# Dense attention of layer 0: head 0's row maxima as a + relu(b - a), differences issued a tile ahead, three relu buffers

## The reference

```python
mod = (_silu(L0_c) @ L0_wmod).reshape(L0_c.shape[0], 6, 1, -1)
h = _layernorm(x, axis=-1) * (1 + ca) + sa
x = x + ga * _L0_attn_ref(h, L0_attn_W_query, L0_attn_W_key, L0_attn_W_val, L0_attn_W_out)
...
        norm = 1.0 / np.sqrt(KEY_DIM)
        Q = jnp.einsum('bsd,hdk->hbsk', q, W_query)
        K = jnp.einsum('bsd,hdk->hbsk', q, W_key)
        V = jnp.einsum('bsd,hdv->hbsv', q, W_val)
        scores = norm * jnp.einsum('hbqk,hbnk->hbqn', Q, K)
        attn = jax.nn.softmax(scores, axis=-1)
        heads = jnp.einsum('hbqn,hbnv->hbqv', attn, V)
        out = jnp.einsum('hbqv,hve->bqe', heads, W_out)
...
```

## Time and profile before

| what | value |
|---|---|
| median of three runs | 1733.46 us |
| the profiled execution's own time | 1726.0 us |
| its span in the trace | 1724.2 us |
| VectorE busy | 1303.6 us (76%) |
| TensorE busy | 1239.0 us (72%) |
| ScalarE busy | 889.7 us (52%) |
| GpSimd busy | 236.1 us (14%) |

### The profile page before, as it was taken

One profiled execution on the slowest core, in us unless ns is written; L12 is line 12 of the kernel. 1 busy time (PEld: TensorE's weight loads), 2 busy tenths in 40 slices (PEclk: granted clock), 3 DMA queues, 4 the chain that ended last, 5 costly groups with the idle time before them and its releaser, 6 DMA issues. The chain is left out here.

```text
span 1724.2 us, 29793 instructions
## 1 busy us (share of the span) xinstructions
PE 1239.0 (72%) x10670; PEld 619.8 (36%) x10674; DVE 1303.6 (76%) x3511; ACT 889.7 (52%) x1757; POOL 236.1 (14%) x275
## 2 busy tenths in 40 slices
PE   7799999999999997574993453060215989824686
PEld 3122222222222223354982342040113547623445
DVE  6999999999999972447237236989897568578873
ACT  4099999999999996412521122020002775502553
POOL 2000000000000000003410324030003321000223
PEclk9599999999999999667995586565656988965668
DMA  2100000011000000000004331000001721031001
GB/s 73 37 14 27 21 21 21 22 28 28 23 21 20 21 2 2 15 29 1 1 1 188 101 84 46 0 0 1 1 0 27 228 68 43 4 116 49 22 22 31
DMA packets 45030, 62.88 MB, mean 36 GB/s; under 512 B 12785, under 2 KB 34356, under 8 KB 44484
## 3 DMA queue, kind: packets, MB, share of 16 engines
q1 hardware_dynamic: 38243, 49.71, 9.7%
q0 software_dynamic: 5440, 10.67, 2.3%
q10 hardware_dynamic: 1200, 0.59, 0.1%
HBM read 34.10 MB, written 13.63 MB: 28 GB/s over the span
## 5 line engine op out<-in xcount | busy, mean ns | idle before, releaser
L842 ACT ACTIVATE l0att_probs<-l0att_ps_sv 128x512 f32<-128x512 f32 x960 | 521.2, 596 | 80.0 <-PE l0att_ps_sv L811 68.1
L888 DVE TENSOR_REDUCE l0att_half_negmax<-l0att_ps_m 128x1 f32<-128x1024 f32 x480 | 547.1, 1216 | 5.6 <-PE l0att_ps_m L741 5.6
L773 PE MATMUL l0att_ps_sv<-l0att_probs,l_V_aug 128*32 128x256 f32 x4096 | 325.3, 392 | 4.8 <-ACT l0att_pv_sb L833 4.7
L811 PE MATMUL l0att_ps_sv<-l_Q,l_K 51*128 51x512 bf16 x992 | 194.5, 388 | 4.0 <-ACT l0att_probs L850 2.4
L741 PE MATMUL l0att_ps_m<-l_K,l_Q 48*128 48x512 bf16 x960 | 185.9, 384 | 11.1 <-DVE l0att_half_negmax L888 7.1
L773 PEld LDWEIGHTS l0att_ps_sv<-l0att_probs,l_V_aug 128*32 128x32 f32 x4096 | 83.0, 108 | 197.4 <-issue 100.9
L811 PEld LDWEIGHTS l0att_ps_sv<-l_Q,l_K 51*128 51x128 bf16 x992 | 48.0, 92 | 207.4 <-ACT l0att_probs L842 188.1
L472 POOL CAST l0att_nm<-l0att_negmax 128x16 bf16<-128x16 f32 x16 | 3.2, 198 | 515.0 <-DVE l0att_negmax L864 515.0
L2862 ACT ACTIVATE l3loc_probs<-l3loc_ps_s 128x320 f32<-128x320 f32 x128 | 48.9, 435 | 36.0 <-PE l3loc_ps_s L2839 35.3
L2040 DVE SCALAR_TENSOR_TENSOR l2spk_lif_v<-l2spk_U 128x64 f32<-128x64 f32 (+1 forms) x368 | 60.8, 207 | 0.0
L741 PEld LDWEIGHTS l0att_ps_m<-l_K,l_Q 48*128 48x128 bf16 x960 | 47.1, 95 | 28.5 <-DVE l0att_half_negmax L888 19.0
(11 more groups left out here) (736 smaller groups left out, 2391.8 us busy)
## 6 DMA issues: line engine op xcount, KB each, us to landing
l_K<-l_kp SPq DMA_DIRECT2D x192, 32.0 KB
l_Q<-l_qp SPq DMA_DIRECT2D x192, 32.0 KB
l1ffn_W<-in_l_expert_w_dram SPq DMA_DIRECT2D x1, 4096.0 KB
l3f_experts_l_w<-in_l_w_dram SPq DMA_DIRECT2D x2, 2048.0 KB
l_sorted_in<-l1ffn_zeros SPq DMA_DIRECT2D x1, 3072.0 KB
l1exp_rows<-l_sorted_in SPq DMA_DIRECT2D x6, 512.0 KB, 5.6
l_sorted_out<-l1exp_y SPq DMA_DIRECT2D x6, 512.0 KB, 4.6
l_Q<-in_local_mask_q_dram POOLq DMA_DIRECT2D x2, 1170.0 KB, 17.3
```

Of the source, the lines that this page charges most:

```text
L773: mm = pe.matmul(ps_v[32 * c:32 * c + 32, cols], V_aug[:, kt, h, :], probs[:, kt % 2, c, cols], start=(kt == 0 and part == 0), stop=(kt == ...
L811: pe.matmul(dst, K[at, h % HEAD_BUFS, c1(kt)], Q[at, h % HEAD_BUFS, c4(2 * pair + i)], start=True, stop=True).then_inc(last_scored[i] if l ...
L842: act.activation(probs[:, kt % 2, c, :], ps_s[:, n % 3, :], ACT.Exp).then_inc(expd, 1)
L888: dve.tensor_reduce(half_negmax[:, h % 2, t, half:half + 1], src, AX_X, ALU.max, negate=True).then_inc(m_read, 1)
```

## The change

Three things are done. First, for query tiles 1 to 15 of head 0, the maximum over the two halves is taken as max(a, b) = a + relu(b - a): TensorE makes b - a in one product over 112 rows of new operands (`Q_both` holds Q and, 64 rows further, -Q; `K_both` holds the keys of the upper half and, 64 rows further, those of the lower half; rows 32 to 63 are cleared first, and 32 to 47 filled again), ScalarE takes the relu into SBUF, and VectorE adds the scores a of the lower half to it and reduces the sum in the same instruction (`tensor_tensor_reduce`). Tile 0 is made as before, with two reductions. The difference of tile u + 1 is issued ahead of the lower scores of tile u, and the relu has three buffers. Second, SyncE loads head 1's rows ahead of the second copy of head 0's. Third, TensorE multiplies the identity by itself five times at the start of the block. GpSimd clears the rows between in the stage ahead.

```diff
@@ stage_project_parts, gpsimd
                 pool.memset(V_aug[:, :, :, L0_K:L0_K + 1], 1.0).then_inc(v_filled, 1)
+                pool.wait_ge(v_filled, 2)
                 if beside is not None:
                     beside(pool)
                 rows_finish(pool, g)
-                pool.wait_ge(v_filled, 2)
@@ stage_l0_attend
+        above = st.sb("above", [P, 3, S // 2])
...
-        first_scores = [ps_m[:, 0, :], ps_m[:, 1, :], ps_sv[:, 0:2, :].rearrange("p b n -> p (b n)"),
-                        ps_sv[:, 2:4, :].rearrange("p b n -> p (b n)")]
+        first_low = [ps_m[:, 0, :], ps_sv[:, 0:2, :].rearrange("p b n -> p (b n)")]
+        first_diff = [ps_m[:, 1, :], ps_sv[:, 2:4, :].rearrange("p b n -> p (b n)")]
@@ sync
-                for piece in high:
-                    load_piece(sp, Q, K, qp, kp, 0, loaded_high, *piece)
                 for h in range(1, L0_H):
...
                         load_piece(sp, Q, K, qp, kp, h, loaded[h % HEAD_BUFS], *piece)
+                    if h == 1:
+                        for piece in high:
+                            load_piece(sp, Q, K, qp, kp, 0, loaded_high, *piece)
@@ tensor
-                pe.wait_ge(loaded_first, LOAD // 2)
-                for n in range(2 * NT):
-                    t, half = n // 2, n % 2
-                    if n >= 4:
-                        pe.wait_ge(first_read, n - 3)
-                    for i in range(2):
-                        pe.matmul(first_scores[n % 4][:, i * BANK:(i + 1) * BANK], Q[0:TERMS, 0, c1(t)],
-                                  K[0:TERMS, 0, c4(2 * half + i)], start=True, stop=True).then_inc(first_filled, 1)
-                pe.wait_ge(first_read, 2 * NT)
+                def first_plain(half):
+                    for i in range(2):
+                        mm = pe.matmul(first_low[half][:, i * BANK:(i + 1) * BANK], Q[0:TERMS, 0, c1(0)],
+                                       K[0:TERMS, 0, c4(2 * half + i)], start=True, stop=True)
+                    mm.then_inc(low_filled, 1)
+                def first_difference(u):
+                    if u >= 2:
+                        pe.wait_ge(above_done, u - 1)
+                    for i in range(2):
+                        mm = pe.matmul(first_diff[u % 2][:, i * BANK:(i + 1) * BANK], Q_both[:, c1(u + 1)],
+                                       K_both[:, c4(i)], start=True, stop=True)
+                    mm.then_inc(diff_filled, 1)
+                def first_lower(u):
+                    pe.wait_ge(low_read, u + 1)
+                    for i in range(2):
+                        mm = pe.matmul(first_low[u % 2][:, i * BANK:(i + 1) * BANK], Q[0:TERMS, 0, c1(u + 1)],
+                                       K[0:TERMS, 0, c4(i)], start=True, stop=True)
+                    mm.then_inc(low_filled, 1)
+                keep_busy(pe, g, first_diff[1], 5)
+                for operand in loaded_first:
+                    pe.wait_ge(operand, LOAD // 4)
+                for half in range(2):
+                    first_plain(half)
+                pe.wait_ge(both_placed, 4)
+                first_difference(0)
+                for u in range(NT - 1):
+                    if u + 1 < NT - 1:
+                        first_difference(u + 1)
+                    first_lower(u)
+                pe.wait_ge(low_read, NT + 1)
@@ scalar
+                act.wait_ge(loaded_first[0], LOAD // 4)
+                act.activation(Q_both[0:TERMS, :], Q[0:TERMS, 0, :], ACT.Identity).then_inc(both_placed, 1)
+                for u in range(NT - 1):
+                    act.wait_ge(diff_filled, u + 1)
+                    if u >= 3:
+                        act.wait_ge(low_read, u)
+                    act.activation(above[:, u % 3, :], first_diff[u % 2], ACT.Relu).then_inc(above_done, 1)
@@ vector
-                for n in range(2 * NT):
-                    dve.wait_ge(first_filled, 2 * (n + 1))
-                    dve.tensor_reduce(half_negmax[:, 0, n // 2, n % 2:n % 2 + 1], first_scores[n % 4], AX_X, ALU.max,
-                                      negate=True).then_inc(first_read, 1)
+                dve.memset(half_negmax[:, 0, 1:NT, 1], -LOWEST).then_inc(missing_set, 1)
+                dve.wait_ge(loaded_first[1], LOAD // 4)
+                dve.tensor_copy(K_both[0:TERMS, :], K[0:TERMS, 0, S // 2:S]).then_inc(both_placed, 1)
+                dve.tensor_copy(K_both[HALF_ROWS:HALF_ROWS + TERMS, :], K[0:TERMS, 0, 0:S // 2])\
+                   .then_inc(both_placed, 1)
+                dve.wait_ge(loaded_first[0], LOAD // 4)
+                dve.tensor_scalar(Q_both[HALF_ROWS:HALF_ROWS + TERMS, :], Q[0:TERMS, 0, :], -1.0, None,
+                                  ALU.mult).then_inc(both_placed, 1)
+                for half in range(2):
...
+                for u in range(NT - 1):
+                    dve.wait_ge(low_filled, u + 3)
+                    dve.wait_ge(above_done, u + 1)
+                    dve.tensor_tensor_reduce(above[:, u % 3, :], first_low[u % 2], above[:, u % 3, :], -1.0, -LOWEST,
+                                             ALU.add, ALU.min, half_negmax[:, 0, u + 1, 0:1]).then_inc(low_read, 1)
@@ layer0_attention
+        def clear_between(pool):
+            for n, operand in enumerate((Q_both, K_both)):
+                pool.memset(operand[32:HALF_ROWS, :], 0.0).then_inc(both_cleared, 1)
+                pool.wait_ge(both_cleared, n + 1)
```

More of the change, by code:

```diff
@@ L615, in load_piece, with stage_l0_attend @@
     eng.dma_start(operand[at:at + TERMS - 5:6, h % HEAD_BUFS, :], parts[part][h:P:L0_H, :]).then_inc(landed, 16)
-def stage_l0_attend(nc, loads, g, V_aug, qp, kp, Q, K, ones_placed, loaded_first, O):
+def stage_l0_attend(nc, loads, g, V_aug, qp, kp, Q, K, ones_placed, loaded_first, Q_both, K_both, O):
     LEAD = 4
@@ L658, in stage_l0_attend @@
         nm_placed = [st.sem("nm_placed0"), st.sem("nm_placed1")]
-        first_filled = st.sem("first_filled")
-        first_read = st.sem("first_read")
+        both_placed = st.sem("both_placed")
+        low_filled = st.sem("low_filled")
+        low_read = st.sem("low_read")
+        diff_filled = st.sem("diff_filled")
+        above_done = st.sem("above_done")
+        missing_set = st.sem("missing_set")
         negmax_ready = st.sem("negmax_ready")
@@ L874, in normalise @@
                                       ALU.mult).then_inc(m_read, 1)
[L876 to L879 removed]
+                dve.memset(half_negmax[:, 0, 1:NT, 1], -LOWEST).then_inc(missing_set, 1)
[7 more added lines that the diff above has]
+                for half in range(2):
+                    dve.wait_ge(low_filled, half + 1)
+                    dve.tensor_reduce(half_negmax[:, 0, 0, half:half + 1], first_low[half], AX_X, ALU.max,
+                                      negate=True).then_inc(low_read, 1)
+                for u in range(NT - 1):
[3 more added lines that the diff above has]
+                                             ALU.add, ALU.min, half_negmax[:, 0, u + 1, 0:1]).then_inc(low_read, 1)
                 for i, what in enumerate(turns):
@@ L954, in layer0_attention @@
         ones_placed = st.sem("ones_placed")
-        loaded_first = st.sem("loaded_first")
+        loaded_first = [st.sem("loaded_first_q"), st.sem("loaded_first_k")]
+        both_cleared = st.sem("both_cleared")
+        Q_both = st.sb("Q_both", [HALF_ROWS + TERMS, S], BF16)
+        K_both = st.sb("K_both", [HALF_ROWS + TERMS, S // 2], BF16)
         for half in range(2):
@@ L966, in first_rows @@
                 if (SPLITS_Q, SPLITS_K)[which][r] == part:
-                    load_piece(sp, Q, K, qp, kp, 0, loaded_first, 0, r, which)
-        stage_project_parts(nc, for_parts, "l0_wqkv", g, 0, "l0proj", V_aug, qp, kp, rows_of_part=first_rows)
-        stage_l0_attend(nc, for_attend, g, V_aug, qp, kp, Q, K, ones_placed, loaded_first, O)
+                    load_piece(sp, Q, K, qp, kp, 0, loaded_first[which], 0, r, which)
+        def clear_between(pool):
+            for n, operand in enumerate((Q_both, K_both)):
+                pool.memset(operand[32:HALF_ROWS, :], 0.0).then_inc(both_cleared, 1)
+                pool.wait_ge(both_cleared, n + 1)
+        stage_project_parts(nc, for_parts, "l0_wqkv", g, 0, "l0proj", V_aug, qp, kp, beside=clear_between,
+                            rows_of_part=first_rows)
+        stage_l0_attend(nc, for_attend, g, V_aug, qp, kp, Q, K, ones_placed, loaded_first, Q_both, K_both, O)
         stage_project_out(nc, for_out, "l0_wout", g, "l0out", O, mod_row(g, 0, GATE_A))
```

3 lines of the change are left out of this document (2 added, 1 removed).

## The result

| | kernel before | changed kernel |
|---|---|---|
| median, first measurement | 1732.06 us (1725.74 to 1736.72, 4 runs) | 1711.88 us (1705.01 to 1722.01, 4 runs) |
| median, second measurement | 1731.53 us (1722.99 to 1734.77, 11 runs) | 1712.89 us (1708.85 to 1715.46, 6 runs) |
| ratio, first and second | | 0.990 (0.9871 to 0.9929), 0.9901 (0.9875 to 0.9926) |

A forecast was written before the change was run, and what follows sets the result against it. VectorE was taken to bound head 0's maxima; their end moving from 71.52 to 56.9 us gains 14.6, the rest costed at nothing, so the median of 1733.46 becomes 1718.9 us, range 1714 to 1729.

The forecast's parts named there:

- What bounds the kernel: Head 0's maxima: VectorE bounds this part, 32 reductions at 1.13 us each from start to start, 36.30 us in all.
- The new start: Opening of the attention stage: first reduction at 36.4 us, 1.2 later than before; first combined instruction at 38.65.
- The bound from below: First reduction of head 0: nothing is gained past 36.0 us, when the first plain scores arrive.
- The tiles: Head 0's 15 tiles: 1.21 us each (bounds 1.13 and 1.25), ending at 56.9 in place of 71.52, a gain of 14.6.
- TensorE at the lower clock: Head 0's tiles: TensorE becomes the bound at 1.71 us a tile, end 64.1, gain 7.4, time 1726.1; chance 0.30.
- Its milder form: Head 0's tiles: TensorE regains its clock after some 7 us, gain 11.9, time 1721.6; shares the lower-clock rival's chance of 0.30.
- The slow instruction: Head 0's tiles: combined instruction as slow as the scan, 2.28 us a tile, time 1734.9; chance 0.05.
- The loads: Head 1's 24 loads go first, landed by 51 us, needed at 56.9; the old order would be a microsecond too late.
- Not seen in the whole: Whole kernel: head 0's gain offset by a median 3.3 us up and a later stage losing 7.2, time 1729.4; chance 0.09.
- rival 3: A later stage, shifted in time, loses 7.2 us to the lower clock and the median stands 3.3 up; 1729.4 us, chance 0.09.
- The time: Whole kernel: the median of the runs, 1733.46 us, less the gain of 14.6 gives 1718.9 us.

The follow-up runs named there:

- two_passes: Changed kernel with the combined instruction taken apart into an addition and a maximum, both over 1024 columns; 1727.74 us, one run.
- no_busy: Changed kernel without the identity products ahead of the first plain product; 1724.48 us, one run.
- busy_2: Changed kernel with two identity products in place of five ahead of the first plain product; 1731.48 us, one run.

## Why the prediction was right, and where it was off

- **What bounds the kernel.** Right. VectorE paces the part before and after, and its halved work is the gain: with the second pass back the stage gained nothing (two_passes). The condition that TensorE keeps its clock was right too, and was worth 10.5 of the 15 us (no_busy).
- **The new start.** Forecast 36.4, 2.35 us after the opening at 34.05; measured 36.81, 1.9 after an opening at about 34.9. The stage opened 0.9 us later, a delay the prediction costed at nothing. GpSimd's work behind the memsets doesn't explain it (it ends at 31.57, ScalarE's last eviction at 34.01), and variants with the same memsets opened between 33.84 and 35.20. It isn't the change's: TensorE was 0.95 us behind at 19.20 already (L411, 18.25 before), because eight products ahead of it took 1.92 us against 1.19 and the next two 1.70 against 1.12, and the change's first instruction, a memset, starts at 23.23. What makes these products long in one execution and short in another stays open. Inside, my terms for VectorE were too large, a K copy 0.42 and 0.35 to 0.45 us from start to start (I took 0.6), the negation 0.68 (1.15). The bound from below, the scores, decided instead: TensorE's identity products (1.35, forecast 1.3) ended at 36.24.
- **The tiles.** Forecast 1.21, measured 1.145, near the lower bound of 1.13. The mis-sized term is the accumulator read: I took 0.08 from a range of 0 to 0.12; it shows as about 0.01, since it runs beside the next instruction's start. Over 14 steps that is 0.9 us, which makes good the later start, by luck: two errors of opposite sign. So the end came at 56.4 (56.9) and the gain in place was 15.1 us (14.6).
- **TensorE at the lower clock.** Did not happen, and the variants show how near it was: with two identity products or none, and for the last tiles with two buffers, a tile took 1.93 us. The price in the rival, 1.71 a tile, was too low by 0.22: I took every matmul at the 0.43 us that a row of one pair gives, and left out that the next pair starts 0.57 behind a pair's second (0.48 in the mean). Its milder form, the clock coming back after some 7 us of full work, did not come either: in no_busy TensorE was busy for 19.69 of 20.60 us and the clock stayed at 0.50 to the loop's end and beyond.
  The Trainium skill ("TensorE: Matmul & The Clock Gate", section "A second HAM failure mode: psum-queue depth-cycling") says that the level can swing to and fro when TensorE idles briefly between groups. No trace here shows that inside this loop: in the variants the clock fell once and stayed down, in the changed kernel it stayed up.
- **The slow instruction.** Ruled out: 1.22 us for 1024 columns, not 2.29. The rule of half rate with two SBUF sources (the Trainium skill, "Vector Engine (DVE) Microarchitecture Reference", section "7. Points that are easy to get wrong") is not tested by the combined instruction, which always has one source in PSUM.
- **The loads.** Forecast a microsecond, measured 1.9.
- **Not seen in the whole.** The mechanism of rival 3 is real (a later stage lost to the lower clock in the first trace), but it strikes before and after alike (twelve of thirteen traces), so nothing says that it moves the medians apart.
- **The time.** The place gained 15.1 us, the stage 14.7 to 15.0; the medians differ by 20.2 and 18.6, and the ratio's interval (12.3 to 22.3 us) holds both, and the stage's 15 as well. I hung my forecast on three runs whose median was 1733.5 and subtracted a gain of 14.6. What lies between 15 and 19 or 20 is not attributed: the second traces of the two kernels differ by 22.7 us in span, 15.6 of it up to the end of attention and the rest in pieces of 1 to 4 us, most of them in layer 3, while the first pair differs by 10.6. Nothing in the change acts there. From the start of the output stage to the end the three traces with the old maxima took 1047.7, 1054.2 and 1054.7 us, the ten others 1045.4 to 1056.2: this wander is as large as what is not attributed, and shows no side. The four runs of the first measurement lay 17 us apart, and a range that took only 2.8 us for spread at the low end was too narrow.

## What to carry to other kernels

When one engine makes two passes over the same data and another is idle, an identity such as max(a, b) = a + relu(b - a) lets matmul and ScalarE do the pairing and leaves one fused pass. A wait thus shortened exposes the next ones by a microsecond or two each (a load queue, a buffer, the clock), so price them in the same stage of the trace and not by single totals, which here wander by more than all of them. And filler for TensorE paid here where it filled the last idle stretch ahead of a loop in which TensorE would be the bound at the lower clock; behind that loop, where it held back products that VectorE waited for, it cost.

## What the runs showed of the hardware

- An accumulator read of 0.08 us behind a 1024-column fused instruction costs about 0.01: the instruction's spacing is 1.145 with it, a plain reduction's 1.13.
- A fused instruction over 1024 float32 columns, with one source in PSUM and one in SBUF, takes 1.22 us, as long as a reduction of one source.
- At the granted clock of 0.50 TensorE's 512-column bfloat16 products start 0.40 us apart inside a pair with the same weights and 0.57 apart from one pair to the next (no_busy).
- Copies with bfloat16 on both sides in SBUF ran far faster than I bounded them: 0.42 us for 1024 columns, 0.68 for 2048, 0.25 ns for each further column, against 1.90 us for 2048 with float32 input. The Trainium skill, "Vector Engine (DVE) Microarchitecture Reference", section "5.1 Performance modes — why throughput varies by op and dtype", says that a one-source copy of 2-byte values within SBUF handles four elements a cycle; by that rule, which I had not weighed, the K copies and the negation would have been costed at about half. The trace agrees with it.
- A short wait of TensorE at a loop's start decided its clock. With 0.78 and 0.91 us of it (busy_2, no_busy) the clock fell to 0.50 within 1.6 us and stayed there for the whole loop, although TensorE was busy for 19.69 of 20.60 us. With 0.12 us or with filler in it (the changed kernel twice, and five variants with the fused maxima) it stayed at 1.00 for at least 15 us of the loop. I can't say from these runs what brings it back.
